# Input norms in two parts around chunk 2's evictions, low halves behind the state sum, end statistics behind the output sums, in a Mamba and FFN block

## What is computed

```
h   = ln(x)                         # per row of 256
xi  = silu(causal_conv4(h @ Wx.T) + b);  z = h @ Wz.T        # 512 channels
B, C, dt = xi @ Wb.T, xi @ Wc.T, softplus(xi @ Wdt.T + b_dt)
state_t = exp(dt_t * a) * state_(t-1) + dt_t * B_t x_t ;  y_t = C_t state_t    # 8 heads of 64 x 64
y   = group_norm_over_sequence(y + d * xi) * silu(z) @ Wout.T
u   = x + ln(y)
out = u + ln(gelu(ln(u) @ binary(w1).T + b1) @ binary(w2).T + b2)
```

## Time and profile before

| | |
|---|---|
| runs of the kernel before | median 1266.62 us of 3 (1266.29 to 1266.91) |
| profiled execution | 1265.6 us |
| its span | 1263.9 us |
| mean granted clock of TensorE | 0.997 |
| PE busy | 1218.3 us, 96% |
| DVE busy | 997.3 us, 79% |
| ACT busy | 878.6 us, 70% |
| POOL busy | 465.5 us, 37% |

### The profile page before, as it was taken

The page is one execution under the profiler, slowest core; times in us unless marked ns, Lnnn a source line. Parts: engine busy times, 40 slices in busy tenths (PEclk is TensorE's granted clock), DMA queues, the critical chain, the costliest instruction groups (busy, mean ns, idle before and its releaser), DMA issues.

```text
span 1263.9 us, 27616 instructions
## 1 busy us (share of the span) xinstructions
PE 1218.3 (96%) x10306; PEld 765.1 (61%) x10306; DVE 997.3 (79%) x2385; ACT 878.6 (70%) x1554; POOL 465.5 (37%) x557
## 2 busy tenths in 40 slices
PE   7999999999999999999999999999999999999896
PEld 5665657565565756656566565756656575564674
DVE  6666877788787796978779787778878789787687
ACT  6675677667776687766966678667787668776365
POOL 2131236142451524416343243623336152441332
PEclk9999999999999999999999999999999999999999
DMA  8011101111020110202111020111112111020001
GB/s 239 1 35 36 34 17 35 43 42 36 18 68 17 35 34 18 68 18 53 26 41 35 18 68 18 35 38 26 55 17 52 34 18 34 18 68 17 2 1 51
DMA packets 91829, 48.09 MB, mean 38 GB/s; under 512 B 63120, under 2 KB 89892, under 8 KB 91696
## 3 DMA queue, kind: packets, MB, share of 16 engines
q1 hardware_dynamic: 91696, 46.33, 14.9%
HBM read 22.72 MB, written 8.39 MB: 25 GB/s over the span
## 4 chain that ended last, share of the span: by engine, by line
PE 76%; DVE 14%; issue 5%; ACT 2%; POOL 2%; DVEq 0%; ACTq 0%; POOLq 0%
PE bank L1728 34%; PE bank L1945 8%; PE bank L1928 8%; PE bank L1837 5%; PE bank L1815 4%; PE bank L1899 3%; DVE xs L1303 3%; PE bank L1905 3%; PE bank L1873 3%; PE bank L1807 2%; PE bank L1860 2%; PE bank L1851 2%; DVE gn_stats L1442 2%; DVE yT L1481 1%; PE bank L1826 1%
## 5 line engine op out<-in xcount | busy, mean ns | idle before, releaser
L937 POOL TENSOR_TENSOR Cd<-Cd,CT 128x512 f32<-128x512 f32 x64 | 93.8, 1465 | 359.8 <-ACT Cd L1180 359.4
L1728 PE MATMUL bank<-sh,WbT 128*128 128x512 f16 x768 | 171.5, 379 | 1.9 <-DVE sh L1308 1.2
L1728 PE MATMUL bank<-sh,WcT 128*128 128x512 f16 x768 | 171.3, 379 | 0.0
L1208 ACT ACTIVATE hf<-bank,vectors,alpha 128x512 f32<-128x512 f32 x128 | 99.0, 776 | 52.0 <-PE bank L1928 30.2
L1303 DVE SCALAR_TENSOR_TENSOR xs<-xi,vectors,xs 128x512 f32<-128x512 f32 x168 | 125.1, 749 | 9.4 <-ACT xs L1085 5.7
L1728 PEld LDWEIGHTS bank<-sh,WcT 128*128 128x128 f16 x768 | 75.2, 98 | 86.6
L1728 PEld LDWEIGHTS bank<-sh,WbT 128*128 128x128 f16 x768 | 72.9, 98 | 87.1 <-DVE sh L1308 6.1
L1928 PE MATMUL bank<-uh,sign1T 128*128 128x512 f16 x512 | 121.6, 380 | 1.8 <-issue 1.7
L1945 PE MATMUL bank<-sign2T,hh 128*128 128x256 f16 x1024 | 117.2, 273 | 1.2 <-DVE hh L1543 1.1
L1945 PEld LDWEIGHTS bank<-sign2T,hh 128*128 128x128 f16 x1024 | 97.8, 98 | 21.7 <-ACT hf L1208 6.5
L868 POOL TENSOR_TENSOR rstd_mid<-var_eps_mid,power 128x4 f32<-128x4 f32 x16 | 16.2, 1011 | 227.3 <-DVE var_eps_mid L1258 227.3
(11 more groups left out here) (235 smaller groups left out, 2600.1 us busy)
## 6 DMA issues: line engine op xcount, KB each, us to landing
xt<-L_attn_input_tensor_dram SPq DMA_DIRECT2D x17, 512.0 KB, 4.1
u<-L_attn_input_tensor_dram SPq DMA_DIRECT2D x15, 512.0 KB, 3.9
out_dram<-u SPq DMA_DIRECT2D x15, 512.0 KB, 3.0
yT<-in_L_ffn_w_dram SPq DMA_DIRECT2D x2, 512.0 KB, 8.8
u<-in_L_ffn_w_dram SPq DMA_DIRECT2D x2, 512.0 KB, 9.3
BT<-in_L_attn_Wx_dram SPq DMA_DIRECT2D x1, 512.0 KB, 5.1
BT<-in_L_attn_Wz_dram SPq DMA_DIRECT2D x1, 512.0 KB, 4.5
zs<-in_L_attn_Wb_dram SPq DMA_DIRECT2D x1, 512.0 KB, 6.2
```

The costliest lines, as they stand in the source:

```text
L937: pool.tensor_tensor(Cd[n % 2][:, :, :], Cd[n % 2][:, :, :], CT[:, :, q * P:(q + 1) * P], ALU.mult)\
L1208: nc.scalar.activation(hf[f % 2][:, :], bank(t, ("H", j, f))[:, :], ACT.Gelu, bias=b1_col[:, f:f + 1], scale=alpha1[:, f:f + 1]).then_inc( ...
L1728: mm = nc.tensor.matmul(bank(t, key)[:, :], w[i][:, k, cols(m)], v[h][:, k, :], start=(a == 0), stop=(a == len(terms) - 1))
```

## The change

The ScalarE step "in_norm" is divided: "in_high" has the waits and the four high halves and stays where "in_norm" was; "in_norm" now has the four plain norms only and stands behind "front" of chunk 2. "xT" and "load" move from behind "back" of chunk 0 to behind "carry" of chunk 1, ahead of "back" of chunk 1. "end_tiles" moves from ahead of "carry" of chunk 1 to behind "back" of chunk 1. No instruction is added or taken away, and TensorE's order is the same.

```diff
-        norm, xT = [(who, "in_norm", nj)], [(who, "xT", nj), (who, "load", nj)]
+        norm, xT = [(who, "in_high", nj)], [(who, "xT", nj), (who, "load", nj)]
...
-        steps += out[1] + own(("back", j, 0)) + xT
+        steps += out[1] + own(("back", j, 0))
...
-        steps += own(("E", j, 2), ("ends", j, 2), ("seg", j, 2), ("front", j, 2), ("score", j, 2)) + end(("end_tiles", j))
-        steps += own(("carry", j, 1), ("back", j, 1), ("E", j, 3), ("ends", j, 3), ("seg", j, 3), ("front", j, 3))
+        steps += own(("E", j, 2), ("ends", j, 2), ("seg", j, 2), ("front", j, 2)) + [(who, "in_norm", nj)]
+        steps += own(("score", j, 2), ("carry", j, 1)) + xT + own(("back", j, 1)) + end(("end_tiles", j)) + own(("E", j, 3), ("ends", j, 3), ("seg", j, 3), ("front", j, 3))
...
-            def input_norm(t, j):
-                if opening(t) and j == 0:
-                    return
+            def input_high(t, j):
                 s, sj = before_block(t, j)
                 act.wait_ge(*conv_out.count(s, (sj + 1) * KI * (TAPS - 1)))
                 act.wait_ge(*uh_hi.count(*(t.ago(1), 1) if j else (t.ago(2), NJ)))
                 for i in range(NQ):
                     normal_high("in", xn_hi, xt[j], t, j, i)
+
+            def input_norm(t, j):
+                if opening(t) and j == 0:
+                    return
                 for i in range(NQ):
                     act.wait_ge(*xn_hi.count(t, j * NQ + i + 1))
                     normal("in", xt[j], xt[j], t, j, i)
```

More of the change, by code:

```diff
@@ L1224, in _ @@
             all_batches(act, {
-                "weights": weights, "silu_table": table(ACT.Silu), "gelu_table": table(ACT.Gelu), "in_norm": input_norm, "ff_norm": ff_norm, "end_norm": end_norm, "first_turn": first_turn, "xi": project_x,
+                "weights": weights, "silu_table": table(ACT.Silu), "gelu_table": table(ACT.Gelu), "in_high": input_high, "in_norm": input_norm, "ff_norm": ff_norm, "end_norm": end_norm, "first_turn": first_turn, "xi": project_x,
                 "z_in": gate_in, "z_silu": gate_silu, "silu": x_silu, "xs_hi": x_high, "dt": step_exp,
```

## The result

The median after the change is **1283.20 us** (4 runs, 1280.76 to 1283.44); before it is 1266.57 us (4 runs, 1266.29 to 1266.91). The ratio is **1.0127, with a 95% interval of 1.0109 to 1.0144**: 16.6 us slower. The profiled execution took 1283.44 us, with a span of 1281.7, which is 17.8 us over the span of before.

What follows compares the result with a forecast made beforehand. TensorE, busy 1218.3 of 1263.9 us, was taken to bound the kernel. First halves 6.25 and second halves 11.65 made 17.9 us, on the median 1266.62 giving 1284.5 us, range 1273 to 1293.

Steps and rivals of the forecast that it cites:

- Part 1: ScalarE's plain norms move behind chunk 2's evictions: costs and gains nothing, TensorE does not notice.
- scores of chunk 2 that start earlier than before: Sign that the forecast is wrong: chunk 2's score product starting earlier than in the kernel before; no size given.
- Part 2: End statistics behind the output sums: chunk 1's state sum waits for GpSimd's product instead; TensorE's 0.28 us wait goes.
- Part 3: Low halves on VectorE between state sum and output sums: output sums and TensorE's transposes come 0.65 us later.
- Part 4: Low halves' transfer issued later: the next batch's projection waits 0.95 us more, a second half costs 1.6 us.
- rival 1: Only the output sums cost, the transfer lands in time: 10.6 us, 1277; chance 0.12.
- Part 5: VectorE's work behind the output sums makes chunk 2's state sum late: 0.1 us per first half (0 to 0.3).
- Batch 0: Batch without end statistics: 1.0 us lost in its first half, 2.05 in its second.
- Rival 2: Low halves slowed by GpSimd, landings near 5.0, state sum 0.3 late: some 36 us, 1302; chance 0.14.
- Rival 3: Faster: state bank wait goes, low halves find room ahead of the output sums: 3.6 us, 1263; chance 0.06.

Runs made afterwards that it cites:

- e2: The changed kernel with the output sums put ahead of the low halves again: 1289.37 us, ratio 1.0180 against the kernel before.
- e3: The changed kernel with the next batch's projection in second halves moved behind chunk 2's state and old-state products on TensorE: 1277.84 us, ratio 1.0090.
- e1b: The kernel before with only the end statistics moved behind the output sums, measured a second time: 1263.16 us, ratio 0.9971.
- e4: The changed kernel with the four plain norms directly behind the high halves again, ahead of chunk 2's evictions: 1286.51 us, ratio 1.0152.
- e4b: The changed kernel with the plain norms directly behind the high halves, run again beside the changed kernel: 1284.38 us, ratio 1.0141.
- e5: The changed kernel with the end statistics ahead of chunk 1's state sum again: 1290.37 us, ratio 1.0184.
- e6: The changed kernel with four additional statistics instructions on VectorE, results unused, ahead of the low halves: 1333.20 us, ratio 1.0520.
- e1: The kernel before with only the end statistics moved behind the output sums: 1261.24 us, ratio 0.9964.

## Why the prediction was right

It named the two waits, the output sums ahead of the transposes and the landing ahead of the projection, and the experiments find both: e2 takes the first away, e3 the second. That 17.9 us were forecast and 17.8 lie between the spans is luck: errors of both signs cancel, and 1.6 us of the 17.8 come from elsewhere. The medians are 16.6 apart. Point by point:

- **Part 1 at nothing: right for the total, not quite in its reason.** "TensorE does not notice" holds in most halves. But with the norms ahead of chunk 2's exponentials, TensorE's scores of chunk 2 start 0.15 to 0.21 us late in two to six of the eight first halves (before 2, e1b 6, e4 3, e4b 5); in the fifteen stretches of after they never do. So the change also gained 0.2 us in batch 0 and 0.15 in batch 7, and one sign that the prediction had named for being wrong, scores of chunk 2 that start earlier than before, appeared in these two halves, at a size that changes nothing. Moved back, the norms run from 668.33 to 670.4, and their reader on VectorE starts at 671.25, as forecast.
- **Part 2, the state sum waits for GpSimd: right.** It was forecast 4.97 us into the half and starts at 4.95. The wait in L1807 is gone. Alone it is worth more than the 0.28 us that I read from the chain (0.38), because the output sums behind the state sum come earlier too; in the change this is used up by part 3. Without it (e5) the transposes come 1.14 us late instead of 0.65.
- **Part 3, +0.65 us: right to the hundredth**, in the start of the low halves (5.29 forecast and measured), in their duration (1.22 against 1.23) and at the transposes. I had taken the shortest of the fifteen durations of before because GpSimd would be elsewhere, and it was: its product starts at 672.16, near the end of the low halves. Where it is not elsewhere, in e6, they take 1.93. The rule of the Trainium skill that I weighed there (GPSIMD Engine Reference, Specifications: SBUF interfaces shared with VectorE, contention with two SBUF inputs) is borne out by both.
- **Part 4: right in its place, too high in its size.** The wait is 0.6 to 0.7 us in these halves, not 0.95. Issue (6.54 us into the half) and due time were as forecast; the term that failed is "3.4 in the median" for the landing. In the seven second halves of after it was 3.1 or 3.2. The median of before went with what ran beside the transfer, and at its new time other things run beside it (last section). There was luck in this as well: the two landings of 4.7 and 4.9 in the trace of after fell into first halves, where nobody waits, while in e3, e4, e4b and e5 one or two fell into second halves, at up to 3.9 us each. The estimate by the Trainium skill (DMA: Bandwidth & Descriptors, Anatomy of one DMA) was worked out with 128 KB, half of what the transfer moves: where it runs alone the queue shows 1056 packets and 0.26 MB, that is 256 KB (row below the list). With these bytes the page's rule gives an estimate of 2.6 us instead of 2.3, and a wait of some 0.1 us at the projection instead of none. It stays too short: no such transfer in any trace here took less than 3.1, and rival 1 did not happen.
- **Part 5, 0.1 us: too small.** TensorE waits 0.18 us for the state sum of chunk 2, and the stage is 0.25 later. My range for it was 0 to 0.3. This makes a first half 0.90 instead of 0.75. Together parts 4 and 5 missed by about +0.15 in a first half and -0.25 in a second.
- **Batch 0: the second half too high, 1.46 against 2.05.** I held that "the whole 1.15 us falls on TensorE", but the low halves had cost something at their old place: they took 2.03 us there, and chunk 2's xdt came behind them. In after xdt starts 2.68 us into the half instead of 4.13, and the state sum 0.4 earlier. So the transposes moved by 0.75, not 1.15, and the low halves with their transfer came 0.4 us earlier than assumed; a landing of 3.1 instead of 3.4 makes up the rest of the difference. The earlier state sum is a gain of taking work away that I had not looked for. In the other halves xdt starts earlier too (1.42 instead of 2.14 us into the half), but there the score product behind it waits for TensorE's scores in any case, and nothing comes of it.

The packets and megabytes of the transfer in the second half of batch 6 of after, where nothing runs beside it (1053.5 to 1057 us):

```profile
q1 hardware_dynamic: 1056, 0.26, 39.9%
```

The terms that were too high take back 2.1 us in second halves, those too low give 0.4 in first ones: 16.2 from the change instead of 17.9. The medians, 16.6 apart, are the better measure of it.

Rival 2 (landings near 5, low halves slowed) is what e3, e4, e4b and e5 show in single halves, and e6 in part: right as a mechanism, absent from the profile of after in second halves. Rival 3 did not happen: the low halves found no room ahead of the sums.

## What to carry to other kernels

When one engine is 96% busy, price a reordering by what stands between a result and that engine's next read of it, not by how much of another engine's waiting it fills: the low halves were free in a hole ahead of chunk 2's data and cost 0.65 us in front of the output sums. A step that starts a transfer carries its landing with it, so look at who reads the data and how much slack is left before moving it by 4.3 us. A change that moves three things is worth taking apart: here one third of it was a gain (e1), one third next to nothing (e4), and one third the whole loss.

## What the hardware showed that I had not expected

**A transfer's landing goes with what else is fetched.** The same 256 KB transposing transfer landed after 3.1 or 3.2 us whenever no packet of the two instruction queues (q8 and q14) began between 0.3 and 3.3 us after its issue. In the traces of eight executions (before, after twice, e2, e3, e4 twice, e5) I found 120 of them. All sixteen that took 4.5 us or more had an instruction fetch that began 1.8 to 2.9 us behind the issue; but so had ten others, which took 3.1 or 3.2, and one that took 3.8. A fetch that began 0.4 to 0.8 us behind the issue goes with 3.3 to 4.0 us in twelve of fourteen cases. Before, five of fifteen transfers had such an early fetch and three a late one with 3.8 to 5.0, hence the median of 3.4 in the earlier trace rows. This is a correlation over traces; no run here moved a fetch on purpose. The load behind the transfer runs beside the end of all the slow ones, and of most fast ones too, so it may have a part in it; why ten escaped stays open. In after and in e3:

```profile
DMA to landing us min/median/max: 3.1/3.1/4.9
```

```profile
q8 instruction: 1, 0.02, 1.0%
...
xh<-xi SPq DMA_TRANSPOSE x1, 4.9
```

The second is the stretch from 440.3 to 446 of e3, whose late projection is shown above. In after the two slow landings fell into first halves, where nobody waits.

**A stall of TensorE can cost more than its length.** In e4 the 2.39 us wait for a landing was followed by 3.4 us at 0.50 of the full clock, that is at 1.2 GHz, the lower of its two levels, and then by full clock again:

```profile
598.33 1.61 PE L1730 MATMUL bank<-xh,WxT 128*128 128x512 f16 x6 [2.39 <-issue]
...
599.87 1.12 PE L1853 MATMUL bank<-xdw,bt 128*64 128x64 f32 x16
```

```profile
593.00:599.50 6.50, 3.36 (x30) 2.34 (x30) 5.30 (x16) 1.76 (x4) 3.70 (x4) 1.00 0.50 124
599.50:602.90 3.40, 3.40 (x43) 2.58 (x43) 0.01 (x1) 2.86 (x6) 0.61 (x1) 0.50 0.01 2
602.90:608.00 5.10, 5.10 (x70) 3.39 (x69) 4.89 (x14) 2.81 (x5) 3.32 (x5) 1.00 0.01 3
```

The waits of 0.7 and 0.9 us in after were never followed by it; those of 2.9 us in e6 were in ten halves of fifteen. In e2, where the projection waits 2.4 to 2.9 us in seven halves, only one was, the shortest of them. So the length of the wait alone does not tell. The Trainium skill describes this (TensorE: Matmul & The Clock Gate, HAM oscillation: a product stream with waits between its groups drops to the lower clock and pays for it in the groups behind). The rows agree, and add that single waits of 2.4 and 2.9 us can do it in an engine that is otherwise busy nearly all the time.

It also accounts for a spread that has nothing to do with the change. Near the end of every trace (batch 7) TensorE waits 3.5 us for ScalarE (the row of L1839 above) and then runs at half clock, for 3.4 us in the profile of before and 6.8 in that of after:

```profile
1173.50:1176.90 3.40, 3.40 (x19) 2.33 (x16) 1.98 (x3) 1.63 (x3) 1.98 (x3) 0.50 0.00 0
```

```profile
1188.30:1195.10 6.80, 5.99 (x36) 4.84 (x38) 2.14 (x4) 3.87 (x8) 4.25 (x4) 0.50 0.01 2
```

A second execution of after had 3.4 us there, and was 1.14 us shorter in that passage. This is the 1.1 us in batch 7 of the first section.
